# A two-layer relational graph convolution on one core: eight relations treated alike, the root product last in each layer

## The reference

```python
def _rgcn_conv(x, src, dst, etype, W, root, b):
    seg = dst * num_rel + etype
    sums = segment_sum(x[src], seg)
    cnt = segment_sum(ones, seg)
    mean = (sums / maximum(cnt, 1.0)[:, None]).reshape(num_nodes, num_rel, -1)
    return einsum('nri,rio->no', mean, W) + x @ root + b

h = relu(_rgcn_conv(x, src, dst, edge_type, W1, root1, b1))
out = _layernorm(x + _rgcn_conv(h, src, dst, edge_type, W2, root2, b2))
```

## Time and profile before

| | us |
|---|---|
| median of 3 runs (1469.45 to 1471.24) | 1470.09 |
| the profiled execution, its time | 1469.78 |
| the profiled execution, its span | 1468.0 |
| PE busy in it | 1451.5 |
| DVE busy | 983.4 |
| ACT busy | 604.9 |
| POOL busy | 572.6 |

### The profile page before, as it was taken

How to read it: one execution, slowest core, us unless ns; L and a number is a source line. 1 busy time by engine, 2 the same in 40 slices (tenths; PEclk the granted TensorE clock), 3 DMA queues, 4 the chain that set the end, 5 groups by cost and what they waited for, 6 DMA issues and landing times.

```text
span 1468.0 us, 23940 instructions
## 1 busy us (share of the span) xinstructions
PE 1451.5 (99%) x8875; PEld 1438.4 (98%) x8875; DVE 983.4 (67%) x1604; ACT 604.9 (41%) x845; POOL 572.6 (39%) x457
## 2 busy tenths in 40 slices
PE   8999999999999999999999999999999999999998
PEld 8999999999999999999999999999999999999997
DVE  8899999857777677898740144545454454539887
ACT  4222344335444443566342233334343333417654
POOL 0000000066777774764306233434242424316553
PEclk9999999999999999999999999999999999999999
DMA  6453321358777786565337465646464656625454
GB/s 200 146 169 124 94 76 43 105 183 267 255 208 247 238 250 188 150 192 165 105 122 216 151 207 170 207 146 218 141 212 151 212 169 189 214 82 149 145 168 132
DMA packets 109595, 249.70 MB, mean 170 GB/s; under 512 B 20183, under 2 KB 83334, under 8 KB 109442
## 3 DMA queue, kind: packets, MB, share of 16 engines
q0 software_dynamic: 32480, 135.65, 31.5%
q1 hardware_dynamic: 77026, 112.88, 23.7%
HBM read 204.47 MB, written 65.49 MB: 184 GB/s over the span
## 4 chain that ended last, share of the span: by engine, by line
PE 94%; DMA 2%; DVE 2%; ACT 1%; issue 1%; SPq 0%; POOL 0%; ACTq 0%; POOLq 0%; DVEq 0%
PE prod L872 72%; PE agg L918 15%; PE agg L1039 2%; PE agg L872 2%; PE prod L863 1%; DMA raw<-y,bucket_index 1%; PE prod L918 1%; DMA y<-y_stage 1%; DVE g_low L1166 1%; PE agg L863 0%; DMA x_rows<-in_x 0%; PE agg L1042 0%; DVE g_low L1170 0%; ACT g_high L705 0%; DVE g_high L1166 0%
## 5 line engine op out<-in xcount | busy, mean ns | idle before, releaser
L872 PE MATMUL prod<-w_high,h_high 128*128 128x384 f32 x2100 | 707.8, 337 | 0.0
L872 PE MATMUL prod<-w_high,h_low 128*128 128x384 f32 x2100 | 702.5, 335 | 0.0
L872 PE MATMUL prod<-w_low,h_high 128*128 128x384 f32 x2100 | 701.8, 334 | 0.0
L590 POOL DMA_INDIRECT raw<-y,bucket_index x346 | 448.7, 1297 | 506.6 <-DVE g_low L1170 249.8
L1170 DVE TENSOR_TENSOR g_low<-raw,g_high 128x768 fp32r<-128x768 f32 x246 | 225.5, 954 | 300.7 <-ACT g_high L708 299.6
L741 ACT ACTIVATE y_stage<-prod 128x384 f32<-128x384 f32 x280 | 137.7, 492 | 679.5 <-PE prod L872 670.3
L872 PEld LDWEIGHTS prod<-w_high,h_high 128*128 128x128 f32 x2100 | 394.3, 188 | 0.3 <-issue 0.2
L872 PEld LDWEIGHTS prod<-w_low,h_high 128*128 128x128 f32 x2100 | 394.5, 188 | 0.0
L872 PEld LDWEIGHTS prod<-w_high,h_low 128*128 128x128 f32 x2100 | 394.2, 188 | 0.0
L708 ACT ACTIVATE g_high<-raw 128x768 fp32r<-128x768 f32 x266 | 211.6, 839 | 64.4 <-PE agg L918 46.2
L918 PE MATMUL agg<-g_high,one_hot 128*128 128x384 f32 x720 | 186.0, 339 | 4.2 <-DVE g_low L1170 2.7
(11 more groups left out here) (178 smaller groups left out, 1002.6 us busy)
## 6 DMA issues: line engine op xcount, KB each, us to landing
y<-y_stage SPq DMA_DIRECT2D x280, 168.0 KB
w_raw<-in_w_all SPq DMA_DIRECT2D x35, 1152.0 KB, 7.2
raw<-y,bucket_index POOLq DMA_INDIRECT x346, 4.8
y<-y_stage SPq DMA_DIRECT2D x280, 19.5 KB
y<-in_x SPq DMA_DIRECT2D x1, 3750.0 KB, 14.0
acc<-in_x POOLq DMA_DIRECT2D x10, 375.0 KB, 4.3
x_rows<-in_x SPq DMA_DIRECT2D x10, 336.0 KB
y<-acc SPq DMA_DIRECT2D x10, 336.0 KB
```

The source lines that it names most:

```text
L590: pool.indirect_dma_start(raw_rows(slot), None, y[0:written * N, :], bass.IndirectOffsetOnAxis(ap=bucket_index[:, at_column:at_column + 1] ...
L872: mm = pe.matmul(to, left[:, k, t * P:(t + 1) * P], right[:, h, k, :], start=(k == 0 and left is h_high and right is w_high), stop=(n == 0 ...
```

## The change

All eight relations are multiplied first, stored and gathered. Each has two gathered tiles for each destination tile, and the overflow of all eight goes to relation 7's four (so that third tile of relation 0, the copy of x to `y`, the store of h to `y`, `average`, its turns and `keep` are gone). Products 0 to 7 are relations 0 to 7 and product 8 is the root product; products 9 to 16 are the relations of layer 2 and 17 is its root product. Both root products now stay in PSUM, and relation 7 is summed onto them (`finish` on PE, ACT and DVE, for both layers). The sums of relation 6 lie in product 7 (16), those of relation 7 in product 8 (17): tiles 0 and 1 after step 4, tile t after step 2t + 2, tile 9 after step 19. Three pairs of PSUM banks rotate in place of four. The sums in products 4 to 6 are as they were. Layer 2's loop now covers seven products (10 to 16).

The first product begins with k = 0 to 2 of its six parts, as soon as half of the weights is split. On DVE the order for tile t of the last product is now: `mark` t+1, `cut_low` of the first tile of t+1, `add` t, `cut_low` of the other three, `moments_of` t, `scale_of` t. The very last tile is summed by halves (`last_bucket`) and added and measured by halves (`last_moments`). The chunks' third matmul has 60 columns in place of 80.

```diff
-    TILES = [FULL] * (R - 2) + [FULL + 1, FULL + OVER]
+    TILES = [FULL] * (R - 1) + [FULL + OVER]
-    ROOT1 = R - 1
-    MEAN1 = R
-    ROOT2 = 2 * R
-    MEAN2 = Q - 1
+    ROOT1 = R
+    ROOT2 = Q - 1
+        def last_part(s):
+            if s < 5:
+                return ((0, 0), (0, 1), (0, 2), (1, 0), (1, 1))[s]
+            if s == STEPS - 1:
+                return 1, T - 1
+            return 1 - s % 2, (s + 1) // 2 - (1 - s % 2)
+        def last_pair(t):
+            return (agg[:, 0, :, 0:HALF], prod[:, 0:2, 0:HALF], prod[:, 2:4, 0:HALF])[t % 3]
+        def finished(s):
+            h, t = last_part(s)
+            return [0, 1] if s == 4 else [t] if s > 4 and h == 1 else []
+        def finishing(layer):
+            def actions(s):
+                todo = [("sum", layer * R + R - 1, R - 1, t) for t in finished(s)]
+                if layer == 0 and s > 4:
+                    todo += [("turn", 1, None, t) for t in ([0] if s == 5 else [n - 1 for n in finished(s)])]
+                return todo
...
# POOL
-            for r in range(1, R - 1):
+            for r in range(R - 1):
                 wait_y(0, r)
...
-            gather_relation(R - 1, R - 1, stop=SOONER)
-            pool.wait_ge(x_copied, 16)
-            gather_relation(R - 2, 0, 1)
-            gather_spilled(0, R - 1)
-            gather_relation(R - 1, R - 1, start=SOONER)
+            gather_spilled(0, R - 1)
+            wait_y(0, R - 1)
+            gather_relation(R - 1, R - 1)
...
# ACT
+            def finish(layer):
+                q, g = (ROOT1, ROOT2)[layer], layer * R + R - 1
+                high_of_unit(q, 1)
+                high_spilled(layer, g)
+                bucket(g, 0)
+                for t in range(T):
+                    if layer == 0 and t == T - 2:
+                        high_of_unit(q + 1, 0, STEPS * q + FIRST_HALF)
+                    if t + 1 < T:
+                        bucket(g, t + 1)
+                    if layer == 0:
+                        relu(t)
+                        if t:
+                            high_of_turn(1, t - 1)
+                    else:
+                        deviation(t)
+                        if t + 1 < T:
+                            norm(t)
...
# PE
+            def last_step(layer, s):
+                h, t = last_part(s)
+                q, stored = (ROOT1, ROOT2)[layer], STEPS * R * (layer + 1)
                 if t == 0:
+                    unit_ready(q, h)
+                    pe.wait_ge(bucket_added, 2 + order_of(layer * R + R - 2, T - 2) + 1)
+                elif t < 3:
+                    pe.wait_ge(y_staged, stored - BANKS + 2 * (t - 1) + h + 1)
                 elif h == 0:
+                    pe.wait_ge(bucket_added, 2 + order_of(layer * R + R - 1, t - 3) + 1)
+                product(q, h, t, last_pair(t)[:, h, :], open_ended=True).then_inc(prod_done, 1)
+            def last_bucket(g, t):
+                pe.wait_ge(one_hot_ready, order_of(g, t) + 1)
+                for c in range(2):
+                    for b, i in enumerate(tile_range(g, t)):
+                        pe.wait_ge(low_ready, NRAW + behind(g) + i + 1)
+                        for part in (g_high,) if folded(g, b) else (g_high, g_low):
+                            mm = pe.matmul(last_pair(t)[:, c, :], one_hot[:, t % 2, b, :],
                                           part[:, split_slot(g, i), c * HALF:(c + 1) * HALF],
                                           start=False, stop=b == tiles(g) - 1, skip_group_check=True)
+                        if c:
+                            mm.then_inc(tile_used, 1)
+                    if not c:
+                        mm.then_inc(half_summed, 1)
...
-                                  keyed[:, c % 2, j, 6 * T:KEYED] if b < FULL else keyed[:, c % 2, j, 0:8 * T],
+                                  keyed[:, c % 2, j, 6 * T:KEYED] if b < FULL else keyed[:, c % 2, j, 0:6 * T],
...
             warm(WARM)
+            pe.wait_ge(first_low, 1)
+            pe.wait_ge(h_low_ready, 2)
+            product(0, 0, 0, prod[:, 0, 0:HALF], ks=range(K // 2))
             turn(0, 1)
-            warm(WARM // 2)
...
# DVE
+            def finish(layer):
+                q, g = (ROOT1, ROOT2)[layer], layer * R + R - 1
+                low_of_unit(unit(q, 1), 1)
+                add_spilled(layer, g)
+                prepare(g, R - 1, 0)
+                for t in range(T):
+                    if layer == 0 and t == T - 2:
+                        low_of_unit(unit(q + 1, 0), 0)
+                    if t + 1 < T:
+                        mark(g, R - 1, t + 1)
+                        cut_low(g, t + 1, 0, 1)
+                    if (layer, t) == (1, T - 1):
+                        last_moments(g, t)
+                        continue
+                    add(g, R - 1, t)
+                    if t + 1 < T:
+                        cut_low(g, t + 1, 1)
+                    if layer:
+                        moments_of(t)
+                        if t + 1 < T:
+                            scale_of(t)
+                    elif t:
+                        low_of_turn(1, t - 1)
+            def last_moments(g, t):
+                dve.wait_ge(half_summed, 1)
+                for c in range(2):
+                    half = slice(c * HALF, (c + 1) * HALF)
+                    if c:
+                        dve.wait_ge(tile_used, NSPLIT + first_of(g, t) + tiles(g))
+                    link(dve.tensor_tensor(acc[:, t, half], last_pair(t)[:, c, :], acc[:, t, half], ALU.add))
+                    ins = dve.bn_stats(stats[:, t % 2, c, :], acc[:, t, half])
+                link(ins)
+                dve.bn_aggr(moments[:, t % 2, :], stats[:, t % 2].rearrange("p c s -> p (c s)")).then_inc(var_ready, 1)
```

More of the change, by code:

```diff
@@ L287, in first_of @@
         def first_of(g, t):
[L289 to L292, removed]
             return behind(g) + tiles(g) * t
         def tile_range(g, t):
-            start = first_of(g, t) - behind(g) if isinstance(g, int) else tiles(g) * t
-            return range(start, start + tiles(g))
-        PAIRED = BEHIND[R - 2]
+            return range(tiles(g) * t, tiles(g) * (t + 1))
+        PAIRED = LAYER
         def raw_slot(g, i):
@@ L902, in step @@
                     pe.wait_ge(*wait)
-                product(q, h, t, prod[:, bank, 0:HALF]).then_inc(prod_done, 1)
+                product(q, h, t, prod[:, bank_of(s), 0:HALF],
+                        ks=range(K // 2 if isinstance(q, int) and q + s == 0 else 0, K)).then_inc(prod_done, 1)
             def bucket(g, t, onto=None):
@@ L1074, in matrix @@
                         else:
-                            bucket(a, t, last_pair(t) if bank is None else None)
-                    if spilled and s == SPILL_STEP[spilled[0]]:
-                        sum_spilled(*spilled)
+                            bucket(a, t)
+            def finish(layer):
+                for s in range(STEPS):
+                    last_step(layer, s)
+                    for what, a, _, t in finishing(layer)(s):
+                        if what == "turn":
+                            turn(a, t)
+                        else:
+                            if (layer, t) == (1, T - 1):
+                                last_bucket(a, t)
+                            else:
+                                bucket(a, t, last_pair(t))
+                    if s == 0:
+                        sum_spilled(layer, layer * R + R - 1)
             pe.wait_ge(pool_step, 3)
@@ L1196, in low_of_turn, with matrix @@
                     low_of_half(u, t, turned(n, hh, t))
[L1198 to L1203 removed]
+            def matrix(q, actions, low_at=((2, 0, K), (12, 0, K))):
+                order = [a[1:] for s in range(STEPS) for a in actions(s) if a[0] == "sum"]
                 ready = n = 0
[L1206 to L1208 removed]
                 for s in range(STEPS):
[L1211 to L1214 removed]
                     for what, *a in actions(s):
@@ L1218, in matrix @@
                             continue
-                        ahead = n + 1 < len(order) and not (s <= cut < order[n + 1][0])
-                        for m in range(ready, n + 1 + ahead):
-                            prepare(*order[m][1])
-                        ready = n + 1 + ahead
+                        for m in range(ready, min(n + 2, len(order))):
+                            prepare(*order[m])
+                        ready = min(n + 2, len(order))
                         n += 1
-                        if what == "sum":
-                            if keep_step:
-                                dve.wait_ge(root_kept, (STEPS if q == MEAN1 else 0) + s + 1)
-                            add(*a)
+                        add(*a)
                     for at, first, stop in low_at:
```

482 lines of the change are left out of this document (127 added, 355 removed).

## The result

The changed kernel takes **1461.74 us** (median of 5 runs, 1460.48 to 1462.46) against 1470.00 before (1469.25 to 1471.24): ratio 0.9944, 95% interval 0.9929 to 0.9958. That is 8.3 us faster. I had forecast 1452.3, in a range from 1446.5 to 1459.5: the sign was right, the size 9.4 short, and the time lies outside the range.

What follows compares the result with a forecast made beforehand. PE was taken to bound the kernel, with 94% of the chain. Terms summed to -17.8 us from a profiled 1469.8, giving 1452.0, plus 0.3 for the runs' median: 1452.3 us, range 1446.5 to 1459.5.

Steps and rivals of the forecast that it cites:

- Steps 1 and 2: PE's transposes and relation 0's sums: 120 transposes go, -13.2 us; two gathered tiles in place of three, -6.9.
- Step 3: Table's chunks: 170 matmuls of 60 columns in place of 80, -1.2 us.
- Step 4: Start of the first product: nine matmuls run early on half the weights, -1.6 us.
- Step 5: Product 7: two-tile sums end PE's waits for gathered tiles, -2.8 us.
- Step 6: Entry to products 8 and 17: tile 1's sum waits for split tiles, +1.95 us in each layer, +3.9.
- Step 7: Middle of product 8: DVE keeps up with PE, 0, up to +1.5 us; a former `relu` hold goes, -0.2.
- Steps 8 and 9: Product 17: an ACT and DVE loop of 8.73 us a tile costs +0.4 in the middle; late DVE lengthens the tail, +3.8.
- A: Product 17: DVE catches up, so the middle's and tail's losses vanish, 1448.1 us; chance 0.20.
- B: Entries to products 8 and 17 come late behind stores, gathers or weight transfers, 1456 to 1460 us; chance 0.18.
- C: Finishing loops of both layers bound by DVE and ACT in every tile, slower than before; chance 0.04.

Runs made afterwards that it cites:

- run 9: Changed kernel with the chunks' third matmul at 80 columns again in place of 60; first step to end of last chunk 111.14 us, against 109.69.
- Run 6: Changed kernel with additions held back, scaling a tile later, first weights in pieces, a step between root products' first two sums, product 9's weights asked for later: 1440.41 us.
- runs 1 and 2: Changed kernel with GpSimd's residual additions held until all h is split, the residual's loads held too or left early: ratios 0.9872 and 0.9854.
- run 8: Changed kernel with additions held back and GpSimd fills of a scratch tile where they stood: low half 2.56 us, four marks 1.17.
- Run 3: Changed kernel with ScalarE's scaling in the last product moved a tile later, behind the next tile's high parts: ratio 0.9915.

## Why the prediction was right in sign and wrong in size

**Steps 1 and 2: right.** The transposes left are the 60 of x and 60 of `acc`. With step 3 they gave 21.3; PE is busy 17.2 us less, and the 4.3 that it lost by the clock in tiles 8 and 9 of product 8 make up for the rest.

**Step 3: right,** -1.7 for -1.2; run 9 shows 1.45 of it, over 16 of the 17 chunks.

**Step 4: wrong.** I wrote that x tile 2 might land late, and looked no further: I moved the transposes of tile 1 behind nine matmuls, but not what SP has queued behind them, tile 3 and the 1152 KB. The traces show +0.7 for -1.6.

**Step 5: right** in product 7, which runs from 579.12 to 655.38 without a wait. That products 4 to 6 would give 2.1 I had not seen: PE waits there 1.0 less (2.67 to 1.66 us), and is busy 1.05 less for the same work. The first may be chance: this stretch is the same in all the changed kernels and takes from 287.0 to 298.5 us, by how long PE waits for gathered tiles. For the second I have no cause; a step takes 3.12 for 3.13 in the layer 2 loop too, some 1 us there.

**Step 6: right.** 22.82 us from product 8's first step to step 5, of which PE's own work is 15.6 + 4.86: 2.35 lost for 1.95, and the same in product 17. Run 6 shows the mechanism in part: a step between the two sums gives 1.9 back, and then a gather is what is late.

**Step 7 is the one that failed.** For the middle of product 8 I wrote "**0**, up to +1.5 if that room goes". The sum of DVE's work for a tile was right: in runs 1 and 2, without the additions, PE has no wait here at all, with the weights in front of the marks, exactly as counted. The loss was one that I put at nothing: what failed is that I took DVE's durations from stretches in which POOL did nothing with SBUF but gather, and never priced that the change takes POOL's two waits away, though the diff says so in three lines; I didn't even show them. I had costed what stands ahead on DVE's own queue, not what a third engine does at that time. The price: 11.3 us, more than the whole miss. The Trainium skill states the rule ("SBUF — State Buffer", Who interferes with whom): VectorE and GpSimd share a pair of ports that one of them holds for a whole instruction; a VectorE instruction in a two-port mode meets it, and one with two inputs in SBUF meets a GpSimd instruction that reads SBUF. The trace agrees: two SBUF inputs slowed (2.55 to 3.98, 1.94 to 4.32), the addition with one input in PSUM not (0.95 and 0.94), and a GpSimd instruction that only writes doesn't slow two-input ones (run 8). The marks are slowed too (0.87 to 6.87), as the rule has it for a two-port mode; that they ran in one, no view shows.

**Steps 8 and 9: right in the mechanism, with luck in one number.** The ten terms of step 8 add up to 8.67, not to 8.73; that is under PE's 8.68, and by it the middle would have cost nothing. The loop takes 8.79, so +0.9 for +0.4; the tail is 13.8 for 14.1, against 10.3 before. Run 3 takes the loop away and both fall.

**The rivals.** A did not come about, since the loop is longer than PE's period, but run 3 made it. B (late entries) was wrong in its reason: the entries are late by what step 6 says, and the time fell just above its interval. C was nearest in kind, "a link of a whole microsecond would have to be missing": there were 9.8 us of them on DVE, but about one tile and not in each. I gave a loss in step 7 no more than 1.5, and the range ended at 1459.5 because B was cut off there. There is luck in the sum too: what step 4 lost against the forecast, 2.3, is nearly made up by the 2.1 of products 4 to 6, which the forecast did not have.

## To carry to other kernels

When a change lets work start earlier, follow what it releases on the engines that nobody waits for: here ten additions on GpSimd, off the critical path before and after, cost 11.3 us by the moment at which they run. A duration read from a stretch holds only beside the same neighbours: look at what GpSimd does with SBUF there and in the place it goes to. In a loop through two engines take each operation that isn't needed by the next link out of the order between them: moving one of 0.83 us by a tile made the loop 1.2 shorter and gave 4.3 in all.

## What the runs showed of the hardware

Short instructions of VectorE fare worst beside a queue of GpSimd additions: four marks that need 0.87 us alone need 6.87. DVE's timeline in narrow windows has the first of them by itself, and then the first two:

```profile
744.23 1.87 DVE L1022 TENSOR_SCALAR one_hot<-column,dst_local 128x128 fp32r<-128x128 bf16 x1
```

```profile
744.23 6.47 DVE L1022 TENSOR_SCALAR one_hot<-column,dst_local 128x128 fp32r<-128x128 bf16 x2
```

So the first ends with the addition under way (742.38 + 3.64), and the second, begun at 746.02, ends only at 750.70, after the two additions that follow: it did not get through in the half microsecond between them. The last two run in POOL's pause, at about 0.3 each. It goes the other way too. POOL's and DVE's timelines in the layer 2 loop, where a gather is issued while the low half of the weights is made:

```profile
878.16 3.09 POOL L521 DMA_INDIRECT raw<-y,bucket_index  x1 [0.30 <-issue]
```

```profile
877.83 2.54 DVE L1000 TENSOR_TENSOR w_low<-w_raw,w_high 128x2304 fp32r<-128x2304 f32 x1
```

The issue of an indirect gather takes 1.00 us alone. Of the 17 that begin during that instruction, 15 take 3.08 to 3.09 and two 2.4; in the layer 2 loop nobody waits for them. And an x tile asked for 1.35 us behind 1152 KB of weights took 8.33 us to land.
